# Preparation moved into the steps of a first attention, and one product moved in a second

## The chip, the cores and the metric

One core of a Trainium2 chip runs the whole program. The metric is the device time of one execution in microseconds. Times and clocks below come from one profiled execution of the kernel before, unless the runs are named.

## The reference, cut to what matters

Eight sequences of 512 tokens with 128 features pass four layers, each with a layer norm ahead and a sum behind:

```python
x = x + attn_a(layernorm(x), w_q, w_k, w_v1, w_v2)   # one head of 64, causal softmax
x = x + ffn(layernorm(x), Wg, W1, W2, W3)            # 8 experts of 352, top 2 of the scores x @ Wg.T
x = x + attn_b(layernorm(x), Q, K, V, W)             # 16 heads of 64, causal softmax
x = x + ffn(layernorm(x), Wg, W1, W2, W3)            # the same weights again
```

An expert computes `silu(x W1^T) * (x W2^T)` and multiplies by `W3^T`; its weight is the score. Everything is float32, and the products are made with pairs: a value is split into a high part (rounded for the fast product, written by ScalarE) and a low part (the rest, by VectorE), and three passes (high x high, high x low, low x high) are summed.

## The kernel before, in words

`build` runs five blocks one after the other: `prepare`, `attention_a`, `experts`, `attention_b`, `experts`. Inside a block each engine has its own instruction list, written out by hand; the lists meet only at semaphores. A list is executed in order, so what stands behind a waiting instruction waits too. At a block's end all engines meet.

**prepare** (L171 to L370). SyncE (L235) issues the loads: x by sequence, the small weights of the first attention, Wg, W1, W2, then Q, K, V, W as `[128, 64, 16]` with rows of 64 bytes, and after seven groups W3 into the place of W1's raw data. GpSimd sets constants and makes `rstd` of the norm (L134, L136). VectorE makes statistics (L123, L127), applies the norm (L146), and writes low parts (L165, L331, L335). TensorE turns `xn` (L154) and the weights by groups of four tiles (L367). ScalarE writes high parts (L160, L349, L352). Eight sequences are normalised in a loop, then Q, K, V are split directly, then come 21 groups: Wg, W1 and W2 (six each), W3 (six), W (two).

**attention_a** (L814). Steps s = -1 to 11. In step s run: scores of sequence s, projections q and k of s + 1, products with the values of s - 1, output of s - 2, and the routing of s - 3 for the experts. Routing is: moments and `rstd` (L447 to L460), `shift` (L466), the rows' norm (`route_apply`, L473), their turn (L649), scores (L664), rank (L683 to L695), count (L706, L709), place (L728 to L742, the last result is `slot`), and eight scatters by GpSimd (L754) to `x_sorted` in DRAM. Before that, SyncE stores zeros over all of `x_sorted` (the blanks, L866), and the scatters of a sequence wait for its chunk. Every result that ScalarE and VectorE split passes a `Ring` of three PSUM banks (L373): the list `order` names the fills in TensorE's order, and a fill waits (`ring_free`) until the fill three places before has been read by its last reader, mostly VectorE's low part.

**experts** (L1028, and again at the end) waits for the table (L810) and the scatters, and works through 142 tiles.

**attention_b** (L1236). 128 heads, one a slot u, in pairs. TensorE's list in a slot is: scores of u, values in two of four slots, in even slots the projection of the next pair, parts of routing, `products(u - 2)` (L554), the first turn of u - 1 (L485), in odd slots `output` of the pair behind (L81 to L83 into `z_bank`), the second and third turn. ScalarE copies each turned part (`b_pt_hi`, L414) between its exponentials (L545), VectorE writes the low parts (`b_pt_lo`, L420) and the maxima (L537), GpSimd multiplies by 1/sum (L1389). The products wait for the low part of the third turn. For the first pair of a sequence, `output` waits for `x_done`: VectorE has added `z_bank` of the sequence before to x (L1577), which it does in slot 5 of 16 of that sequence, behind the third maximum.

```python
def output(pair):
    b, p = divmod(pair, NP)
    pe.wait_ge(y_lo_done, pair + 1)
    if p == 0:
        wait(pe, x_done, b)
    three_passes(nc, z_bank[:], [w[:, p * P:p * P + P] for w in g.b_w], [part[:] for part in y_parts],
                 p == 0, p == NP - 1).then_inc(z_full, 1)
```

Of the kernel before, what the change touches and what calls it, by code (L numbers as in the profile page):

```python
# [4 lines left out]
F32 = mybir.dt.float32  # L5
# [6 lines left out]
P = 128  # L12
# [158 lines left out]
def prepare(nc, g, ins):  # L171
# [3 lines left out]
    with ExitStack() as ctx:  # L175
        sb = lambda n, s, d: ctx.enter_context(nc.sbuf_tensor(n, s, d))
        pb = lambda n: ctx.enter_context(nc.psum_tensor(n, [P, 512], F32))
        n = Norm(nc, ctx, "n0")
        a_raw = sb("a_raw", [P, 3, P], F32)
        v2_raw = sb("v2_raw", [P, D], F32)  # L180
        wg_raw = sb("wg_raw", [NE, D], F32)
        wg_rest = sb("wg_rest", [P, NE], F32)
        f_raw = [sb("f_raw0", [P, NE * HW], F32), sb("f_raw1", [P, EC * P], F32)]
        w3_raw = f_raw[0]
        qkv_raw = [sb(f"qkv_raw{i}", [P, KD, NH], F32) for i in range(4)]
        w_perm = sb("w_perm", [P, NH * KD], F32)
        sem = lambda n: g.spent.append(ctx.enter_context(nc.semaphore(n))) or g.spent[-1]
        norm_bank = [pb(f"norm_bank{i}") for i in range(2)]
        bank = [pb(f"prep_bank{i}") for i in range(4)]
        x_in = [sem(f"x_in{b}") for b in range(NB)]  # L190
        a_in = sem("a_in")
        wg_in = sem("wg_in")
        f_in = [sem(f"f_in{i}") for i in range(3)]
        b_in = [sem(f"b_in{i}") for i in range(4)]
# [4 lines left out]
        perm_done = sem("perm_done")  # L199
        padded = sem("padded")  # L200
        turned = sem("turned")
        turned_hi = sem("turned_hi")
        turned_lo = sem("turned_lo")
# [8 lines left out]
        for i, (parts, scale) in enumerate(((g.b_q, 1.0 / 128), (g.b_k, 1.0), (g.b_v, 1.0))):  # L212
            raw = qkv_raw[i][:].rearrange("p q h -> p h q")
            hi, lo = (part[:].rearrange("p (h q) -> p h q", h=NH) for part in parts)
            direct.append((raw, scale, hi, lo, b_in[i], 16))


        by_tile = lambda part: part.rearrange("p (k w) -> p k w", w=P)
        groups = [([(wg_raw[:], g.ident[0:NE, 0:NE], NE)], wg_in, 16, g.wg[:].unsqueeze(1), wg_rest[:].unsqueeze(1))]
        for i, parts in enumerate((g.w1, g.w2)):  # L220
            for j in range(0, EC, 4):
                m = min(4, EC - j)
                groups.append(([(f_raw[i][:, (j + k) * P:(j + k) * P + P], g.ident[:], P) for k in range(m)], f_in[i], 16,
                               *(by_tile(part[:, j * P:(j + m) * P]) for part in parts)))
# [1479 lines left out]
```

## Time and profile before

| | |
|---|---|
| median of 3 runs | 1491.33 us (1491.08 to 1492.69) |
| the profiled execution | 1491.82 us, of which the span of its instructions is 1490.1 us |
| mean granted clock of TensorE | 0.919 |
| busy: TensorE, VectorE, ScalarE, GpSimd | 81%, 74%, 64%, 51% of the span |
| TensorE clock in 40 equal slices | `9986656999959999999999999999999998599996` |
| share of the DMA engines in 40 slices | `9391011222125656555555556565555652122215` |
| stores of zeros in the first attention | 64, 260 KB each |

A slice is 37.3 us; a digit is tenths, 9 is 90% or more. The first two slices are the preparation, the next four the first attention, with the zeros stored in slices two and three. The clock digits 5 and 6 stand in the first attention's later half and at two changes of stage; slices 12 to 33 are the long attention. A granted clock of 1.00 is 2.4 GHz, 0.50 is 1.2 GHz, and a number between them is the mean of a stretch with both.

### The profile page before, as it was taken

What the parts mean: (1) busy time and instruction counts of PE and PEld (TensorE: products, weight loads), DVE (VectorE), ACT (ScalarE), POOL (GpSimd) and SP (SyncE); (2) the same over time, 40 slices, a digit from 0 to 9 for tenths busy, and PEclk for the clock granted to TensorE, in tenths of its full rate; (3) what the DMA queues carried; (4) which work ended last, traced back from release to release, by engine and by line L of the source; (5) the groups of instructions that cost most, each with busy time, mean ns of one, the idle gap of its engine ahead of it and who ended that gap; (6) DMA issues with size and microseconds to landing.
All of it is one profiled execution on the core that took longest, in us unless ns stands there. A gap on an engine that the chain in (4) does not pass through costs nothing. (4 is left out here: it accounts for less than half of the span.)

```text
span 1490.1 us, 28115 instructions
## 1 busy us (share of the span) xinstructions
PE 1212.1 (81%) x7865; PEld 1037.6 (70%) x7865; DVE 1099.0 (74%) x2826; ACT 946.7 (64%) x2522; POOL 757.9 (51%) x950
## 2 busy tenths in 40 slices
PE   1587734999928898988998999999999997299992
PEld 1476633999817777777777777777777776199992
DVE  5666534777727788888888888888888886277774
ACT  1554421444418788888888888889898886154440
POOL 3004463444405555576575576675765765334443
PEclk9986656999959999999999999999999998599996
DMA  9391011222125656555555556565555652122215
GB/s 182 102 379 61 29 38 45 62 60 61 40 71 128 142 128 140 130 133 139 125 129 136 127 136 141 131 153 128 135 135 127 139 131 47 31 63 60 61 52 175
DMA packets 122658, 165.15 MB, mean 111 GB/s; under 512 B 40164, under 2 KB 84079, under 8 KB 122512
## 3 DMA queue, kind: packets, MB, share of 16 engines
q1 hardware_dynamic: 109648, 144.34, 41.1%
q0 software_dynamic: 8640, 16.93, 3.6%
q10 hardware_dynamic: 4224, 2.10, 0.5%
q8 instruction: 71, 1.16, 0.3%
q14 instruction: 75, 0.61, 0.1%
HBM read 26.59 MB, written 36.96 MB: 43 GB/s over the span
## 5 line engine op out<-in xcount | busy, mean ns | idle before, releaser
L1389 POOL TENSOR_TENSOR b_probs<-b_probs,b_recip 128x128 f32<-128x128 f32 (+3 forms) x512 | 352.1, 717 | 294.8 <-DVE b_recip L1622 294.8
L420 DVE TENSOR_TENSOR b_pt_lo<-b_ring,b_pt_hi 128x512 fp32r<-128x512 f32 (+1 forms) x384 | 229.7, 598 | 104.1 <-ACT b_pt_hi L414 101.7
L545 ACT ACTIVATE b_probs<-b_s_bank,b_neg_max 128x256 f32<-128x256 f32 (+3 forms) x512 | 266.2, 530 | 47.9 <-DVE b_neg_max L537 47.9
L1227 POOL DMA_INDIRECT y_rows<-f_y_sb,f_dest x142 | 138.8, 978 | 193.0 <-DVE f_y_sb L1200 185.2
L537 DVE TENSOR_REDUCE b_neg_max<-b_s_bank 128x1 f32<-128x256 f32 (+3 forms) x512 | 219.2, 479 | 11.1 <-PE b_s_bank L529 10.9
L1437 PE MATMUL b_s_bank<-b_stack 128*128 128x256 f32 (+3 forms) x1024 | 208.0, 338 | 13.8 <-DMA b_stack<-b_qk 7.5
L414 ACT ACTIVATE b_pt_hi<-b_ring 128x512 fp32r<-128x512 f32 (+1 forms) x384 | 204.8, 534 | 14.4 <-PE b_ring L485 11.3
L485 PE MATMUL b_ring<-ident,b_probs 128*128 128x128 f32 x1280 | 190.4, 281 | 13.3 <-DVE b_qk L420 12.6
L554 PE MATMUL b_pv_bank<-b_pt_hi,b_v 128*128 128x512 f32 (+3 forms) x512 | 161.4, 327 | 45.8 <-DVE b_pt_lo L420 45.5
L1170 ACT ACTIVATE f_hid_hi<-f_hid_bank 128x384 fp32r<-128x384 f32 x142 | 69.8, 491 | 160.1 <-PE f_hid_bank L1123 135.3
L485 PEld LDWEIGHTS b_ring<-ident,b_probs 128*128 128x128 f32 x1280 | 140.6, 141 | 41.6 <-DVE b_qk L420 21.1
L1437 PEld LDWEIGHTS b_s_bank<-b_stack 128*128 128x128 f32 x1024 | 139.4, 191 | 24.8 <-ACT b_probs L545 9.8
L554 PE MATMUL b_pv_bank<-b_pt_lo,b_v 128*128 128x512 f32 (+3 forms) x512 | 146.4, 323 | 0.0
L554 PEld LDWEIGHTS b_pv_bank<-b_pt_hi,b_v 128*128 128x128 f32 x512 | 96.7, 189 | 65.2 <-DVE b_pt_lo L420 57.2
L1206 DVE TENSOR_TENSOR f_hid_lo<-f_hid_bank,f_hid_hi 128x384 fp32r<-128x384 f32 x142 | 79.2, 558 | 61.9 <-ACT f_hid_hi L1170 61.8
L1135 PE MATMUL f_y_bank<-w,f_hid_hi 128*128 x426 | 116.4, 342 | 3.7 <-DVE f_y_sb L1200 2.9
L545 ACT ACTIVATION_READ_ACCUMULATOR b_probs<-b_s_bank,b_neg_max 128x1 f32 x512 | 107.5, 210 | 0.0
L554 PEld LDWEIGHTS b_pv_bank<-b_pt_lo,b_v 128*128 128x128 f32 x512 | 96.9, 189 | 7.8
L1135 PEld LDWEIGHTS f_y_bank<-w,f_hid_hi 128*128 128x128 f32 x426 | 79.9, 188 | 25.6 <-issue 21.2
L754 POOL DMA_INDIRECT x_sorted<-a_r_rows,a_r_slot x64 | 62.3, 974 | 67.4 <-DVE a_r_slot L742 51.0
L1137 PE MATMUL f_y_bank<-w,f_hid_lo 128*128 x426 | 94.9, 223 | 0.0
L414 ACT ACTIVATE b_qk<-b_ring 128x512 fp32r<-128x512 f32 x128 | 72.5, 593 | 32.0 <-DMA b_stack<-b_qk 21.8
(298 smaller groups left out, 3024.2 us busy)
## 6 DMA issues: line engine op xcount, KB each, us to landing
b_stack<-b_qk SPq DMA_DIRECT2D x128, 384.0 KB, 5.0
b_stack<-b_qk SPq DMA_DIRECT2D x128, 256.0 KB, 4.8
x_sorted<-a_blank SPq DMA_DIRECT2D x64, 260.0 KB, 3.5
b_stack<-b_qk SPq DMA_DIRECT2D x128, 128.0 KB, 4.9
f_xs<-x_sorted SPq DMA_DIRECT2D x142, 65.0 KB
b_yc<-y_rows SPq DMA_DIRECT2D x16, 256.0 KB, 4.2
f_yc<-y_rows SPq DMA_DIRECT2D x16, 256.0 KB, 5.1
y_rows<-f_y_sb,f_dest POOLq DMA_INDIRECT x142
```

The costliest lines, as they stand in the source:

```text
L414: nc.scalar.activation(dst, src(rg.of(key)), ACT.Copy).then_inc(rg.hi_done, 1)
L420: nc.vector.tensor_tensor(dst, src(rg.of(key)), hi.bitcast(F32), ALU.subtract).then_inc(rg.lo_done, 1)
L485: last = nc.tensor.transpose(rg.of(keys[k])[:, to:to + P], probs[:, P_AT[i] + j * P:P_AT[i] + j * P + P], ident[:])
L537: nc.vector.tensor_reduce(sc.neg_max[:, i:i + 1], s_tile(sc, i), AX.X, ALU.max, negate=True).then_inc(sc.max_done, 1)
L545: nc.scalar.activation(probs[:, P_AT[i]:P_AT[i] + (i + 1) * P], s_tile(sc, i), ACT.Exp, bias=sc.neg_max[:, i:i + 1], accum_out=sums[:, i:i ...
L554: last = nc.tensor.matmul(pv_bank[:, j * P:T], v_at(j), pt[part][:, PT_AT[j]:PT_AT[j] + T - j * P], start=(j == 0 and part == 0), stop=(j ...
L1135: nc.tensor.matmul(y_bank[:, 0:2 * P], hi[:, c * P:c * P + P], w3[:, bass.ds(at, 2 * P)], start=c == 0, stop=False)
L1137: last = nc.tensor.matmul(y_bank[:, 0:P], lo[:, c * P:c * P + P], w3[:, bass.ds(at, P)], start=False, stop=c == HC - 1)
L1206: nc.vector.tensor_tensor(lo[:], hid_bank[i % 2][:, 0:HW], hi[:].bitcast(F32), ALU.subtract).then_inc(hid_lo_done, 1)
L1227: nc.gpsimd.indirect_dma_start(out=g.y_rows, out_offset=bass.IndirectOffsetOnAxis(dest[:, i:i + 1], 0), in_=y_sb[i % NY][:], in_offset=Non ...
L1389: nc.gpsimd.tensor_tensor(part, part, recip[:, i:i + 1].to_broadcast([P, (i + 1) * P]), ALU.mult).then_inc(probs_done, 1)
L1437: nc.tensor.matmul(s_tile(sc, i), stack[u % 2][:, 0, i * P:i * P + P], stack[u % 2][:, part, 0:(i + 1) * P], start=(i == S_GROUPS[group][0 ...
```

## The change

Of `prepare`, only the constants, the first attention's own weights and the norm of sequence 0 stay, with the issues of the loads of x, Wg, W1 and W2. The norms of sequences 1 to 7, the turns and splits of Wg, W1, W2, W3 and W, the splits of Q, K, V and the loads of Q, K, V, W and W3 go into the steps of `attention_a`: Wg ahead of all, three groups a step in steps 3 to 8 (`group(s, j)`), Q and K after step 9's routing, W and V in step 10. They use the ring of `attention_a` (its `order` grows accordingly). The loads of W3 and then Q, K, V, W are issued by SyncE behind all blanks. The lists of all five engines in a step are in a new order.

TensorE's list in a step (s before and after; the waits are inside the named functions):

```diff
             def body(s):
+                if s == NB + 2:
+                    permuted(0)
+                    permuted(1)
                 if live(s):
-                    scores(s)
-                if live(s + 1):
-                    project(s + 1)
+                    scores(s, 0)
+                    scores(s, 1)
+                if 0 < s + 1 < NB:
+                    norm_turn(s + 1)
+                if live(s - 2):
+                    output(s - 2)
+                if group(s, 0) is not None:
+                    weights(group(s, 0))
+                if live(s):
+                    scores(s, 2)
+                if live(s - 3):
+                    route_turn(nc, pe, g, rt, rg, s - 3)
                 if live(s - 1):
                     products(s - 1)
                 if live(s - 3):
-                    route_turn(nc, pe, g, rt, rg, s - 3)
-                if live(s - 2):
-                    output(s - 2)
+                    route_score(nc, pe, g, rt, rg, s - 3)
+                if live(s + 1):
+                    project(s + 1)
                 if live(s):
                     values(s)
                 if live(s - 3):
-                    route_score(nc, pe, g, rt, rg, s - 3)
+                    route_count(nc, pe, g, rt, rg, s - 3)
+                for j in (1, 2):
+                    if group(s, j) is not None:
+                        weights(group(s, j))
                 if live(s):
                     pe.wait_ge(sc.exp_done, s * QT + QT)
                     for k in range(len(PT_BANKS)):
                         head_transpose(nc, pe, rg, turns(s), probs, k, g.ident)
-                if live(s - 3):
-                    route_count(nc, pe, g, rt, rg, s - 3)
```

VectorE's new list in a step:

```diff
+                if s == NB + 2:
+                    for i in range(2):
+                        split_lo(nc, dve, rg, ("wb", i), perm_group(i)[1][1], perm_group(i)[1][0], in_tiles(4))
+                if 0 < s + 1 < NB:
+                    norm_apply(s + 1)
+                if live(s - 1):
+                    head_transposed_lo(nc, dve, rg, turns(s - 1), pt, 0)
+                    head_transposed_lo(nc, dve, rg, turns(s - 1), pt, 1)
                 if live(s - 3):
                     shift(nc, dve, g, rt.m, s - 3)
...
+                if live(s - 1):
+                    head_transposed_lo(nc, dve, rg, turns(s - 1), pt, 2)
+                if live(s):
+                    head_max(nc, dve, sc, s, 0)
+                if 0 < s + 1 < NB:
+                    split_lo(nc, dve, rg, ("norm", s + 1), g.xn_lo[:, tokens(s + 1)], g.xn_hi[:, tokens(s + 1)])
+                if live(s):
+                    head_max(nc, dve, sc, s, 1)
+                if live(s - 2):
+                    add(s - 2)
+                if group(s, 0) is not None:
+                    weights_lo(group(s, 0))
+                if live(s):
+                    head_max(nc, dve, sc, s, 2)
+                if live(s - 2):
+                    moments(nc, dve, g, rt.m, s - 2, x_done, (s - 1) * QT)
+                if live(s - 3):
+                    route_scored(nc, dve, g, rt, rg, s - 3)
+                if 0 < s + 2 < NB:
+                    norm_stats(s + 2)
+                if live(s - 3):
+                    route_rank(nc, dve, g, rt, rg, s - 3)
...
                 if live(s - 3):
                     route_place(nc, dve, g, rt, rg, s - 3)
-                if live(s - 2):
-                    add(s - 2)
-                    moments(nc, dve, g, rt.m, s - 2, x_done, (s - 1) * QT)
+                for j in (1, 2):
+                    if group(s, j) is not None:
+                        weights_lo(group(s, j))
+                if s == NB + 1:
+                    dve.wait_ge(b_in[3], 16)
+                    nc.vector.tensor_scalar(w_perm.rearrange("p (h v) -> p h v", h=NH),
...
```

GpSimd's list, and SyncE's added loads:

```diff
+            for s in range(-2, NB + 3):
+                if live(s - 2):
+                    rstd(nc, pool, g, rt.m, s - 2)
+                if live(s - 3):
+                    pool.wait_ge(blanked[(s - 3) % 2], ((s - 3) // 2 + 1) * NE * 16)
+                    for j in range(0, 6):
+                        route_scatter(nc, pool, g, rt, s - 3, j)
+                if 0 < s + 3 < NB:
+                    norm_rstd(s + 3)
+                if live(s - 2):
+                    route_dest(nc, pool, g, rt, s - 2)
+                if live(s - 3):
+                    for j in range(6, NK * QT):
+                        route_scatter(nc, pool, g, rt, s - 3, j)
...
+            ring_filled(sp, rg, ("w", 5))
+            sp.dma_start(w3_raw.rearrange("p (e h) -> p e h", e=NE)[:, :, 0:EH],
+                         W3.rearrange("e d h -> d e h")).then_inc(g.f_in[3], 16)
+            ring_filled(sp, rg, ("v", 3))
+            for i, w in enumerate((Q, K, V)):
+                sp.dma_start(qkv_raw[i], w.rearrange("q d h -> d q h")).then_inc(b_in[i], 16)
+            sp.dma_start(qkv_raw[3], W).then_inc(b_in[3], 16)
```

ScalarE's list puts the second and third copy of the turns of s - 1, the norm's high part, `route_apply`, the first group and `route_turned` ahead of the exponentials; q, y and k stand behind the second exponential group, and groups two and three and the first copy of the turns at the end.

In the long attention, TensorE's list:

```diff
+                if pair_behind(u, 5) is not None:
+                    output(pair_behind(u, 5))
                 if alive(u - 2):
                     products(u - 2)
                 if alive(u - 1):
                     pe.wait_ge(probs_done, u * QT)
                     head_transpose(nc, pe, rg, turns(u - 1), probs[(u - 1) % 2], 0, g.ident)
-                if pair_behind(u, 5) is not None:
-                    output(pair_behind(u, 5))
-                if alive(u - 1):
                     head_transpose(nc, pe, rg, turns(u - 1), probs[(u - 1) % 2], 1, g.ident)
                     head_transpose(nc, pe, rg, turns(u - 1), probs[(u - 1) % 2], 2, g.ident)
```

The experts are untouched.

## Rows read from the trace of the kernel before

**Rows 1.** Windows by stage: stretch, length, busy by engine, clock, DMA share, GB/s

```profile
16.40:68.10 51.70, 21.86 (x105) 17.51 (x105) 38.22 (x115) 20.21 (x31) 8.76 (x15) 0.97 0.67 108
68.10:93.30 25.20, 22.90 (x152) 18.95 (x152) 16.02 (x31) 16.29 (x45) 0.53 (x1) 1.00 0.96 353
93.30:185.30 92.00, 72.20 (x378) 62.60 (x377) 54.61 (x193) 40.09 (x105) 37.45 (x42) 0.68 0.32 113
185.30:227.40 42.10, 16.23 (x83) 15.01 (x81) 17.14 (x85) 8.89 (x19) 27.53 (x30) 0.50 0.12 38
449.00:1262.00 813.00, 740.02 (x4810) 616.11 (x4810) 690.65 (x1581) 693.04 (x1864) 507.87 (x653) 0.99 0.57 131
```

**Rows 2.** Timeline at the two ends of the preparation: start, us, instruction, idle before

```profile
11.45 4.39 SPq L250 DMA_DIRECT2D f_raw<-in_L_ffn_W_dram  x2
...
16.24 0.66 DVE L165 TENSOR_TENSOR xn_lo<-norm_bank,xn_hi 128x512 f32 x1
...
66.55 1.28 DVE L335 TENSOR_TENSOR wb_w_lo<-prep_bank,wb_w_hi 128x512 fp32r<-128x512 f32 x2
...
68.11 0.53 POOL L873 MEMSET a_blank<- 128x520 f32 x1 [14.22 <-POOLq L175]
```

**Rows 3.** Windows of 4 us over the loads; columns as in rows 1

```profile
20.00:24.00 4.00, 1.13 (x5) 0.71 (x4) 2.92 (x15) 0.67 (x2) 1.29 (x3) 1.00 1.10 269
24.00:28.00 4.00, 1.12 (x4) 0.72 (x4) 2.87 (x14) 0.82 (x2) 1.35 (x4) 1.00 1.64 114
```

**Rows 4.** Instruction groups of VectorE until 68.1 us: count, busy us, mean ns, idle before

```profile
L146 DVE TENSOR_SCALAR n_xn<-x_tok,n_mv,n_rstd 128x128 f32 (+1 forms) x32 | 8.9, 342 | 2.3 <-POOL n_rstd L136 2.3
...
L123 DVE BATCH_NORM_STATS2 n_stats<-x_tok 128x6 f32 (+1 forms) x32 | 7.0, 283 | 2.0 <-DMA x_tok<-in_L_attn_a_x_dram 2.0
L165 DVE TENSOR_TENSOR xn_lo<-norm_bank,xn_hi 128x512 f32 (+1 forms) x8 | 5.5, 688 | 7.1 <-ACT xn_hi L160 7.1
...
L127 DVE BATCH_NORM_AGGREGATE n_mv<-n_stats 128x2 f32<-128x6 f32 x32 | 3.0, 156 | 0.3
```

**Rows 5.** Timeline: the last slot of the first attention

```profile
227.20 0.21 DVE L742 TENSOR_REDUCE a_r_slot<-a_r_of_place 128x8 int32<-128x64 f32 x1
```

**Rows 6.** Window of one step with routing; columns as in rows 1

```profile
130.00:148.00 18.00, 13.84 (x78) 11.47 (x77) 10.81 (x39) 7.97 (x21) 9.03 (x10) 0.69 0.09 30
```

**Rows 7.** Timeline: turns by TensorE at a granted clock of 0.50

```profile
108.71 2.37 PE L485 MATMUL a_ring<-ident,a_probs 128*128 128x128 f32 x10
```

**Rows 8.** Waits, 449 to 1233 us: who for whom, total us, times, longest

```profile
PE b_pv_bank L554 <- DVE b_pt_lo L420: 38.7, 55, 1.2
...
ACT b_qk L414 <- DMA b_stack<-b_qk: 20.2, 21, 2.8
...
PE b_z_bank L81 <- DVE x_tok L1577: 9.5, 7, 1.4
```

**Rows 9.** Timeline of an ordinary odd slot of the long attention

```profile
820.69 0.50 PE L554 MATMUL b_pv_bank<-b_pt_hi,b_v 128*128 128x512 f32 x1 [0.34 <-DVE b_pt_lo L420]
...
822.01 0.63 PE L485 MATMUL b_ring<-ident,b_probs 128*128 128x128 f32 x4
...
822.68 0.60 ACT L414 ACTIVATE b_pt_hi<-b_ring 128x512 fp32r<-128x512 f32 x1
```

**Rows 10.** Timeline of slot 5 of a sequence in the long attention

```profile
984.10 0.50 PE L554 MATMUL b_pv_bank<-b_pt_hi,b_v 128*128 128x512 f32 x1 [0.29 <-DVE b_pt_lo L420]
...
986.66 0.68 DVE L1577 TENSOR_TENSOR x_tok<-x_tok,b_z_bank 128x512 f32<-128x512 f32 x1
986.67 0.60 ACT L414 ACTIVATE b_pt_hi<-b_ring 128x512 fp32r<-128x512 f32 x1
...
987.49 0.47 PE L81 MATMUL b_z_bank<-b_y_hi,wb_w_hi 128*128 128x512 f32 x1 [1.43 <-DVE x_tok L1577]
...
988.90 0.60 ACT L414 ACTIVATE b_pt_hi<-b_ring 128x512 fp32r<-128x512 f32 x1 [0.96 <-PE b_ring L485]
```

**Rows 11.** Timeline: the first instruction behind the first attention

```profile
243.57 0.16 POOL L1221 MEMSET f_dest<- 128x71 int32 x1 [5.54 <-POOLq L830]
```

More of the change, by code:

```diff
@@ L356, in _ @@
             pe.wait_ge(consts, 16)
[L357 to L368 removed]
+            norm_transpose(nc, pe, g, n, 0, norm_bank)
 class Ring:
@@ L391, in of @@
         return self.bank[self.at[key] % len(self.bank)]
-HI_ONLY = ("rows",)
+HI_ONLY = ("rows", "wg")
 LO_ONLY = ("scores", "counts", "table")
@@ L811, in plan_table, with attention_a, group @@
     nc.vector.tensor_scalar(pl.valid[:], bank[:, 2 * P:3 * P], g.index[:, 0:1], None, ALU.is_gt).then_inc(pl.table_done, 1)
-def attention_a(nc, g, pl):
+def attention_a(nc, g, pl, ins):
+    Q, K, V, W, W3 = ins[5], ins[6], ins[7], ins[8], ins[12]
+    NG, PER = 18, 3
     turns = lambda b: [("turn", b, k) for k in range(len(PT_BANKS))]
-    order = []
-    for s in range(-1, NB + 4):
+    def group(s, j):
+        return PER * (s - 3) + j if s >= 3 and 0 <= PER * (s - 3) + j < NG else None
+    order = [("wg", 0)]
+    for s in range(-1, NB + 3):
+        if s == NB + 2:
+            order += [("wb", 0), ("wb", 1)]
+        order += [("norm", s + 1)] if 0 < s + 1 < NB else []
+        order += [("w", group(s, 0))] if group(s, 0) is not None else []
+        order += [("rows", s - 3), ("scores", s - 3)] if live(s - 3) else []
         order += [("q", s + 1), ("k", s + 1)] if live(s + 1) else []
-        order += [("rows", s - 3)] if live(s - 3) else []
         order += [("v", s)] if live(s) else []
-        order += [("scores", s - 3)] if live(s - 3) else []
+        order += [("counts", s - 3)] if live(s - 3) else []
+        order += [("w", group(s, j)) for j in (1, 2) if group(s, j) is not None]
         order += turns(s) if live(s) else []
-        order += [("counts", s - 3)] if live(s - 3) else []
     order += [("table", 0)]
@@ new lines, in norm_turn, with weights @@
+            def norm_turn(b):
+                pe.wait_ge(n_xn_done, b * QT)
+                ring_free(pe, rg, ("norm", b))
+                for t in range(QT):
+                    last = nc.tensor.transpose(rg.of(("norm", b))[:, t * P:t * P + P], n_xn[:, t * D:t * D + D], g.ident[:])
+                last.then_inc(rg.filled, 1)
+            def weights(i):
+                pe.wait_ge(g.f_in[1 + i // 6], 16)
+                if i // 6 == 2:
+                    pe.wait_ge(padded, 1)
+                ring_free(pe, rg, ("w", i))
+                for k, src in enumerate(weight_group(i)[0]):
+                    last = nc.tensor.transpose(rg.of(("w", i))[:, k * P:k * P + P], src, g.ident[:])
+                last.then_inc(rg.filled, 1)
@@ L895, in project, with permuted @@
+            def permuted(i):
+                pe.wait_ge(perm_done, 1)
+                ring_free(pe, rg, ("wb", i))
+                for k, src in enumerate(perm_group(i)[0]):
+                    last = nc.tensor.transpose(rg.of(("wb", i))[:, k * P:k * P + P], src, g.ident[:])
+                last.then_inc(rg.filled, 1)
             def project(b):
+                if b:
+                    pe.wait_ge(rg.lo_done, rg.lo["norm", b])
                 for name, w in (("q", g.a_wq), ("k", g.a_wk)):
```

275 lines of the change are left out of this document (145 added, 130 removed).

## The prediction

> **What bounds the kernel now.** I first cut the span into stages [rows 1] and asked of each which engine has no idle time and what ends the idle time of the others. The reader should see five stages. Until 16.4 us only sequence 0 is normalised, its low part `xn_lo` last [rows 2]. From 16.4 to 68.1 us the kernel prepares: VectorE is busy for 38.2 of 51.7 us, TensorE for 21.9, and nothing of the attention runs. From 68.1 to 227.4 us the first attention runs, its last `slot` at 227.2 us [rows 5]. The experts follow, and from 449 us the long attention, where the span mostly goes: 813 us with TensorE at 91%, VectorE and ScalarE at 85%, so no engine has much room there and the order decides. In the first attention it is otherwise. Until 93.3 us (steps 0 to 2, TensorE at full clock) VectorE is busy 16.0 of 25.2 us; in the next 92.0 us, five steps with routing, only 54.6, and the clock is 0.68; in the last 42.1 us (steps 8 to 10) 17.1, the clock at 0.50. One such step of 18.0 us has 10.8 us of VectorE and 8.0 of ScalarE in it [rows 6]: it is bound by a chain across engines (place, add, moments, `rstd` on GpSimd, shift, rows, turn, scores, rank, count, place) and not by work. So the preparation stage is a stretch that can be covered, and the first attention has idle time to cover it with.
>
> **The change in the first attention.** *Start.* The part that stays in `prepare` ends with `xn_lo` of sequence 0. Before, that split ran at 16.24 us, behind the statistics of sequence 1 [rows 2]; without them it can follow `xn_hi` at once, by about 15.8. SyncE is then the last: its last load of W1 and W2 is issued at 15.84 [rows 2]. With 0.3 us for the change of blocks (as from 67.83 to 68.11 before) and some slack, the attention's first instruction comes at 16.4 instead of 68.1: 51.7 us less. Everything else is what comes back into the steps.
>
> *Added work of VectorE.* For one sequence: four statistics 0.87, four aggregates 0.38, four applications 1.11, one low part 0.69, together 3.0 us; for one weight group, which has the shape of the latter, again 0.69 [rows 4], busy time over eight sequences. With three groups, a step of 3 to 5 gets 3.0 + 2.1 = 5.1 us. ScalarE gets a copy of 0.6 us for each, 2.4 in such a step, on top of 8.0: it stays under VectorE. GpSimd gets 1.25 us beside 9.0 [rows 6]. Its queue is passed in order: `norm_rstd` of sequence s + 3 stands between the sixth and the seventh scatter and waits for statistics that VectorE makes a step later, so two scatters and the next `rstd` wait behind it. Their result is wanted at the next step's head; by my count of the instructions between, VectorE has 7 us of work in that time and GpSimd 5: covered, by 2 us.
>
> *Steps -1 to 2.* They get 1.2 + 3 x 3.0 = 10.2 us of VectorE, and had 9.2 idle [rows 1]. But `norm_apply` stands at the head of the step, and project(s + 1) now waits for turn, high and low part of the same sequence. I take 7.5 us more (0 if all falls into idle time; 15 if ScalarE's and TensorE's parts, 0.6 and 1.1 us for each of three, are added in full too).
>
> *Steps 3 to 7.* VectorE has 10.8 + 5.1 = 15.9 us in steps 3 to 5. The new order puts shift and application first, the sums and moments in the middle and place last, so that the routing chain of one sequence lies beside scores and products of another; I take the fill that the long attention reaches with such an order, 0.86 of the time there (0.85 with its ends, [rows 1]), so 18.5 us each. Step 6 has no statistics left: 14.6 / 0.86 = 17. Step 7 has no norm and no q, k: 11.5 / 0.86 = 13.4; the old step took 18.5; the mean, 16. Together 88.5 instead of 92.0: 3.5 less. Bounds: 74 (VectorE never idle) and 113 (the old time plus all that is added).
>
> *Steps 8 to 10.* 17.1 us of VectorE plus three groups (2.1), w_perm (1.1), three direct low parts (1.9 each) and two groups of W: 27.3, or 31.7 at 0.86. The old time is 42.1, where the clock of 0.50 and the serial chain count; the mean, 37: 5 less. Bounds 32 and 52.
>
> *Loads.* x, W1 and W2 (5 MB) come at some 270 GB/s until about 24 us [rows 3], and the blanks (64 x 260 KB) queue behind them; at the 353 GB/s of before [rows 1] they end near 72 us. The first scatter is due at about 66 and needs only the first chunk. W3 and Q, K, V, W follow the blanks on SyncE's queue and are wanted in steps 7 and 9: hidden by two steps or more. If that cover went, the four strided loads (2 MB at 114 GB/s, [rows 3]) would cost some 18 us once.
>
> Sum: -51.7 + 7.5 - 3.5 - 5.1 = **-52.8 us**; the stretch behind the last slot (scatters, table) stays.
>
> *The clock.* TensorE has 1.00 granted in steps 0 to 2, where it is busy for 22.9 of 25.2 us, and 0.68, then 0.50, later, where it waits longer [rows 1]. The five steps get four turns for the norm and twelve for the weights, so its waits get shorter, and I expect it nearer to 1.0. The Trainium skill ("TensorE: Matmul & The Clock Gate", "HAM oscillation — how this bites in real kernels") says that idle gaps between bursts throw TensorE back to its lower clock; the trace agrees, and by that rule the added work half pays for itself.
>
> **The change in the long attention.** In odd slots `output(pair)` (three products of 512 columns, 0.70 us) moves from behind the first turn to in front of `products`. *What it fills:* TensorE stands 38.7 us in 55 slots at the products, waiting for `pt_lo` [rows 8]; the output now runs in that time. *What it delays:* the ScalarE copy of the first turn starts as soon as that turn ends in most odd slots [rows 9]: products wait 0.34 us, start at 820.69, and ScalarE starts at 822.68, 0.04 after the turn's end. With the output in front they start 0.36 later, and so does ScalarE. Over all odd slots, 0.70 minus the wait where that is positive, less the slack of 0.6 us that 14 of the 62 have in the timeline, comes to 7 us. *What it gives back:* all of TensorE's work after the second turn is earlier by the filled wait, up to 0.6 us a pair, which shortens ScalarE's waits for the stack's DMA (20.2 us in all, [rows 8]) and for turns; I take a third, 9 us.
>
> *The added wait.* For the first pair of a sequence, `output` waits for `x_done`, the sum of the sequence before; seven such waits, 9.5 us [rows 8]. Row by row [rows 10]: products start at 984.10, the copy of the first turn at 986.67, the sum is made at 986.7 and the output starts at 987.49. After the change the products are queued behind that wait: output 987.49 to 988.2, products to 989.6, first turn to 990.2. ScalarE's copy comes 3.6 us later, its exponential of 0.7 after it, and the second copy at 991.5 instead of 988.90 (which now needn't wait for its turn): the slot grows by **2.6 us**. Seven times: 18. Bounds: 0, if the following slots take it up; 25 (7 x 3.6) if nothing is regained.
>
> Sum: 7 - 9 + 18, taken as **+15.5 us** (bounds -15 and +28).
>
> Together -52.8 + 15.5 = -37.3 on the profiled execution's 1491.8 us (span 1490.1 and 1.7 around it), which is 0.5 over the median: **1454.0 us**.
>
> **The rivals.**
> *A, the wait for `x_done` is taken up* (0.2). For it: after the stall TensorE has the second turn ready at once, and later slots have TensorE waits. Against: ScalarE and VectorE are the loop that sets the slot. Then 1491.3 - 52.8 - 2 = 1436 us.
> *B, half of VectorE's moved work is not covered* (0.2). The old stage's idle time is idle because of a chain, and the ring of three banks, which now passes 20 more fills, ties the three engines together. Of 38 us moved 19 come back and nothing is won in the steps: 1491.3 - 51.7 + 19 + 15.5 = 1474 us.
> *C, the block of `prepare` ends only when the loads of W1 and W2 have landed* (0.1): then the attention starts near 24 us [rows 3] and the change does not do what its start says; 7.5 us more, 1461 us. At the end of the first attention, where scatters are under way, the next block does start 5.5 us late [rows 11].
> *D, slower: TensorE stays at its lower level and becomes the bound* (0.05). A step's 13.8 us of TensorE at a mean clock of 0.69 [rows 6] are 19.1 at 0.50, and the sixteen turns added, at 0.24 us each there (ten in 2.37 us, [rows 7]), 3.8: 22.9, and with the 4.2 us that TensorE now waits in a step, 27. For steps 3 to 8 that is 6 x 27 = 162 instead of 100 in my sum (88.5 and 12): 1454 + 62 = 1516 us. It decides from about 24 us a step on. Against it: a TensorE busy for 91% of the time had the full clock in both places where that was so [rows 1].
>
> **How the numbers follow.** My forecast, 0.45, holds 1440 to 1468. The predicted time is its own. Range 1430 to 1480: it takes in A to C and leaves out D, B's worse half and a first attention filled better than 0.86 together with A. A measurement of this kernel can tell about 0.2%, 3 us, from no change: faster 0.94 (all but D and a piece of B), slower 0.05, the same 0.01.
>
> **What would show it.** Right: `a_blank` is set near 16.4 us; scores of step 3 near 49 us; slots every 18.5, later 16 and 12 us, the last near 174 us; granted clock above 0.8 in steps 3 to 7; in the long attention TensorE idles before the `z_bank` product and not before `pv_bank`, seven slots of a sequence's head are 2.6 us longer and others equal. Wrong: a start at 24 us (C), steps over 20 us with VectorE below 75% (B), a clock of 0.5 with TensorE above 90% (D), no longer head slots (A). Most would go wrong with the ring: if a fill waits for a low part that stands late on VectorE, all three engines stop, which none of my sums has priced.

## The result

The changed kernel takes **1478.64 us** (median of 4 runs, 1477.18 to 1479.69) against 1491.2 us (1489.81 to 1492.69) of the kernel before: a ratio of 0.9915, with a 95% interval of 0.9898 to 0.9932. It is 12.6 us faster where I forecast 37. The sign and the range held, the size didn't: a third of the forecast gain is there. The range held with nothing to spare, 1.4 us inside its upper end.

Windows by stage of the changed kernel: stretch, length, busy by engine (TensorE, its weight loads, VectorE, ScalarE, GpSimd), granted clock, DMA share, GB/s. The stretches answer to those of [rows 1]: steps -1 to 2, steps 3 to 7, steps 8 to 10, and the long attention from its first 1/sum to its last.

```profile
16.40:49.00 32.60, 27.54 (x168) 22.65 (x168) 29.21 (x97) 19.40 (x50) 6.35 (x10) 0.97 1.06 360
49.00:136.20 87.20, 68.83 (x434) 60.38 (x434) 68.98 (x244) 48.51 (x118) 42.09 (x48) 0.83 0.67 149
136.20:177.10 40.90, 20.43 (x115) 18.16 (x114) 27.05 (x84) 19.33 (x32) 29.32 (x29) 0.58 0.12 38
401.20:1236.40 835.20, 761.19 (x4781) 616.66 (x4780) 687.87 (x1574) 688.08 (x1855) 502.37 (x646) 0.98 0.56 127
```

The same stretch of the long attention in the kernel before:

```profile
449.50:1251.40 801.90, 733.27 (x4780) 610.41 (x4780) 686.32 (x1573) 688.16 (x1854) 501.83 (x646) 1.00 0.58 132
```

The reader sees a first attention whose last `slot` ends 50.3 us earlier (177.1 against 227.4), and a long attention that is **33 us longer** with VectorE and ScalarE busy for the same time to 2 us. TensorE is busy for 28 us more with the same instructions, and its clock fell from 1.00 to 0.98. So the first part came nearly as forecast, and most of it was given back in the second. The waits of the long attention in the changed kernel (who for whom, total us, times, longest) say where:

```profile
PE b_z_bank L81 <- DVE x_tok L1691: 20.8, 7, 3.1
```

```profile
ACT b_pt_hi L329 <- PE b_ring L400: 36.2, 13, 5.5
```

The seven waits for `x_done` went from 9.5 [rows 8] to 20.8 us, and ScalarE's waits for turned parts, the first turn behind such a wait among them, went from 8.9 to 36.2 us (13 waits in both) and now reach 5.5 us. One of them in the timeline (start, us, instruction, idle before), beside [rows 10]:

```profile
957.69 0.68 DVE L1691 TENSOR_TENSOR x_tok<-x_tok,b_z_bank 128x512 f32<-128x512 f32 x1
...
958.52 0.77 PE L81 MATMUL b_z_bank<-b_y_hi,wb_w_hi 128*128 128x512 f32 x1 [2.97 <-DVE x_tok L1691]
...
959.08 0.63 PE L82 MATMUL b_z_bank<-b_y_lo,wb_w_hi 128*128 128x512 f32 x1
...
959.94 0.63 PE L469 MATMUL b_pv_bank<-b_pt_hi,b_v 128*128 128x512 f32 x1
...
961.98 1.28 PE L400 MATMUL b_ring<-ident,b_probs 128*128 128x128 f32 x10
...
962.64 0.60 ACT L329 ACTIVATE b_pt_hi<-b_ring 128x512 fp32r<-128x512 f32 x1 [4.82 <-PE b_ring L400]
```

The wait of 2.97 us is as worked out. What isn't in my sum is the duration behind it: a product of 512 columns takes 0.63 us, where it takes 0.40 at the full clock (L82 in the lines of e5 below). TensorE came out of the wait at half its clock.

### The profile page after: what moved, and what is told of

Same layout as the page of the kernel before. It is cut to its first block and busy times, and to the rows that moved or that the text cites. A ratio compares the mean times of both kernels' runs of the same rounds, so it can differ in the third digit from the quotient of the medians.

```text
span 1476.9 us, 28006 instructions
## 1 busy us (share of the span) xinstructions
PE 1224.8 (83%) x7865; PEld 1032.5 (70%) x7865; DVE 1099.4 (74%) x2819; ACT 948.5 (64%) x2522; POOL 762.3 (52%) x949
## 5 line engine op out<-in xcount | busy, mean ns | idle before, releaser
L1552 PE MATMUL b_s_bank<-b_stack 128*128 128x256 f32 (+3 forms) x1024 | 211.5, 340 | 19.1 <-DMA b_stack<-b_qk 10.0
L1552 PEld LDWEIGHTS b_s_bank<-b_stack 128*128 128x128 f32 x1024 | 140.5, 192 | 35.5 <-DMA b_stack<-b_qk 15.5
L469 PE MATMUL b_pv_bank<-b_pt_lo,b_v 128*128 128x512 f32 (+3 forms) x512 | 150.4, 330 | 0.0
L469 PEld LDWEIGHTS b_pv_bank<-b_pt_hi,b_v 128*128 128x128 f32 x512 | 99.8, 195 | 41.5 <-DVE b_pt_lo L335 32.3
L469 PEld LDWEIGHTS b_pv_bank<-b_pt_lo,b_v 128*128 128x128 f32 x512 | 100.0, 195 | 9.0
L1742 DVE TENSOR_TENSOR b_y<-b_pv_bank,b_y 64x512 f32<-64x512 f32 x128 | 87.4, 683 | 4.1 <-ACT b_y L1663 2.2
```

Of the source, the lines that this page charges most:

```text
L469: last = nc.tensor.matmul(pv_bank[:, j * P:T], v_at(j), pt[part][:, PT_AT[j]:PT_AT[j] + T - j * P], start=(j == 0 and part == 0), stop=(j ...
L1552: nc.tensor.matmul(s_tile(sc, i), stack[u % 2][:, 0, i * P:i * P + P], stack[u % 2][:, part, 0:(i + 1) * P], start=(i == S_GROUPS[group][0 ...
L1742: nc.vector.tensor_tensor(y[row:row + KD, :], pv_bank[0:KD, :], y[row:row + KD, :], ALU.add).then_inc(y_done, 1)
```

## The experiments

The texts put down ahead of each run name theories by a letter. In the first group T says that the added wait makes the loss, R that what the first attention leaves behind makes it, S that moving the output costs by itself.

**Whose order costs what.** First, each part alone, and two ways to take only the wait away, all on one chip, where the kernel before took 1493.0 us.

e1 puts the old order back into the long attention:

```diff
-                if pair_behind(u, 5) is not None:
-                    output(pair_behind(u, 5))
                 if alive(u - 2):
                     products(u - 2)
 ...
                     head_transpose(nc, pe, rg, turns(u - 1), probs[(u - 1) % 2], 0, g.ident)
+                if pair_behind(u, 5) is not None:
+                    output(pair_behind(u, 5))
+                if alive(u - 1):
 ...
```

> The kernel after with the long attention's TensorE list as it was before (output behind the first turn); the first attention stays changed. Theory T: the gain of the first attention (its last slot came 50.3 us earlier) is all there, and it was given back in the long attention by the wait for the sum of x in front of the products, whose seven occurrences make the 33 us by which that stage is longer. Then this kernel takes 1491.2 - 49 = 1442 us, 1440 to 1446, and the long attention is 802 us from its first to its last reciprocal. Rival R: the long attention is slower because of what the first attention leaves (placement of data, DMA, clock); then it stays near 835 us and the time near 1475.

Measured: 1455.03 us, ratio 0.9738 (0.9709 to 0.9767), 38 us faster than the kernel before, not 49, and above the 1440 to 1446 expected; its long attention 807.4 us. Theory T holds for 27.6 of the 33 us; 5.5 us stay with the order of before, so R isn't all wrong. The other half of the missing 11 us is in the first attention: with the same code its last slot is at 182.2 us here, 5.3 later than in the result's trace.

e2 is the kernel before with that diff turned round: the new order of the long attention, and nothing else.

> The kernel before with the new TensorE list of the long attention alone. Theory T: the order alone costs what the long attention lost in the changed kernel, 33 us: 1524 us, 1519 to 1528. Rival R (cost from what the first attention leaves): about 1491. My forecast's own sum of this part was +15.5: 1507.

Measured: 1518.16 us, ratio 1.0167 (1.014 to 1.0195): the new order alone makes the old kernel **slower by 25 us**, its long attention 826.5 instead of 801.9. That is just under T's 1519 to 1528, whose 33 us had the 5.5 of e1 in them. The two ratios multiply to 0.990, the result's 0.9915 to within their intervals: the parts add up.

e3 keeps the output in front for seven pairs of eight:

```diff
+                behind = pair_behind(u, 5)
+                if behind is not None and behind % NP != 0:
+                    output(behind)
 ...
                     head_transpose(nc, pe, rg, turns(u - 1), probs[(u - 1) % 2], 0, g.ident)
+                if behind is not None and behind % NP == 0:
+                    output(behind)
+                if alive(u - 1):
 ...
```

> The kernel after, but the output of the first pair of a sequence (which waits for the sum of x) stands behind the first turn as before; the seven other pairs keep it in front of the products. Theory T: all of the loss is the wait, and the move of the other pairs is worth about nothing or a little (my forecast had 7 lost, 9 won): 1441 us, 1437 to 1446. Rival S: the move itself costs in every odd slot, by the delay of ScalarE's copy (my forecast's 7 us, without what it gives back) or more: 1450 and above.

e4 leaves the output in front and moves VectorE's sum, from behind the three maxima to ahead of them:

```diff
             for u in slots:
+                if leaving(u, Z_ADD) is not None:
+                    added(leaving(u, Z_ADD))
                 if alive(u):
                     head_max(nc, dve, sc, u, 0)
 ...
-                if leaving(u, Z_ADD) is not None:
-                    added(leaving(u, Z_ADD))
```

> The kernel after, with VectorE's sum of x put ahead of the three maxima of slot 5 instead of behind them; the output stays in front of the products. Its input was ready before the slot began, so the sum ends at about 1.4 us after the slot's start instead of 4 and TensorE doesn't wait. Theory T: the loss is that wait and the fall of TensorE's clock behind it: 1442 + 7 x 0.7 at most for maxima that come later, so 1442 to 1448. Rival S (the move of output costs by itself): 1455 and above.

Measured: e3 1453.58 (0.9724, 0.9694 to 0.9754), e4 1452.87 (0.9721, 0.9693 to 0.9749); long attention 807.8 and 807.1 us against e1's 807.4. e1 and e3 are 13 us over the times that I wrote, e4 5 to 11, and e3's time taken by itself lies where S expected it. But e1, which moves no output, is as long, and the three agree with one another: S falls, the move of 56 outputs is worth 0.4 us (e3's long attention against e1's), and seven waits make all of the 27 us.

**What the seven waits cost.** In the changed kernel's own trace one of the seven waits, that of 3.12 us at 533.4 us, was not followed by a fall of the clock. The 3.2 us behind the output's start in the next sequence (first line) and in this one (second):

```profile
638.50:641.70 3.20, 3.18 (x9) 2.72 (x10) 0.00 (x0) 0.00 (x0) 0.00 (x0) 0.50 0.63 157
533.40:536.60 3.20, 3.19 (x22) 2.98 (x23) 0.00 (x0) 0.54 (x2) 0.00 (x0) 1.00 0.56 134
```

Nine instructions at 0.50, twenty-two at 1.00. A slot is measured from one 1/sum of VectorE to the next. Here are those around the wait with the full clock, in the changed kernel,

```profile
527.84 0.18 DVE L1736 RECIPROCAL b_recip<-b_sums 128x4 f32<-128x4 f32 x1
537.36 0.18 DVE L1736 RECIPROCAL b_recip<-b_sums 128x4 f32<-128x4 f32 x1
544.01 0.18 DVE L1736 RECIPROCAL b_recip<-b_sums 128x4 f32<-128x4 f32 x1
```

and in the kernel before:

```profile
574.01 0.18 DVE L1622 RECIPROCAL b_recip<-b_sums 128x4 f32<-128x4 f32 x1
580.05 0.18 DVE L1622 RECIPROCAL b_recip<-b_sums 128x4 f32<-128x4 f32 x1
587.80 0.18 DVE L1622 RECIPROCAL b_recip<-b_sums 128x4 f32<-128x4 f32 x1
```

The slot with the full clock took 9.51 us, those with a fall 10.5 to 11.6, where the kernel before has 6.05; the slot behind is back from 7.74 to 6.65 us (in the last sequence, whose slots are shorter, from 7.34 to 6.09). So the wait by itself is 9.51 + 6.65 - 6.05 - 7.74 = 2.4 us, and a fall 1.4 to 2.1 more (the last sequence's slot is 9.01 us without one, in e5 below; the smallest price of a fall, in e8, is 0.9). The Trainium skill ("TensorE: Matmul & The Clock Gate", "HAM oscillation — how this bites in real kernels") says that gaps between bursts bring the slower clock back; the traces agree, though the gaps of its example are longer than most of these: in the three traces with waits of 2.7 to 3.4 us at this place (changed, e2, e8), 18 of 21 were followed by it, and none of the 35 waits of 0.92 to 1.44 us in the five of the old order (before, e1, e6, e9, e10), nor of the 14 of up to 1.48 us in e3 and e7.

The length of one wait doesn't decide alone. At other places of the long attention seven falls stand behind waits of 1.73 to 2.00 us, one of them in e5:

```profile
639.57 1.03 PE L400 MATMUL b_ring<-ident,b_probs 128*128 128x128 f32 x6 [1.82 <-DVE b_qk L335]
```

e10 and e11 have a fall each behind a wait of 1.19 us with two shorter ones ahead of it, while 2.10 us in e7 and 2.29 us in e8 kept the clock at 1.00.

The second group ran on another chip, where the kernel before took 1485.65 us, with the changed kernel again as e8. Theory C says that the fall of the clock is part of the price; N that only the wait counts; P that the price goes with the wait's length. e5 fills the wait with products whose result is overwritten:

```diff
+                behind = pair_behind(u, 5)
+                if behind is not None and behind % NP == 0 and behind > 0:
+                    wait(pe, y_done, u - 2)
+                    for k in range(11):
+                        nc.tensor.matmul(pv_bank[:], g.b_w[0][:, 0:P], g.b_q[0][:, 0:T], start=True, stop=True)
                 if pair_behind(u, 5) is not None:
                     output(pair_behind(u, 5))
```

> The kernel after, with 11 products of 512 columns into the free bank of the products, whose result is overwritten, put in front of the output that waits for the sum of x, seven times in all. In the changed kernel TensorE stands there for 3.0 us and its granted clock is 0.50 for the 3.2 us behind, so the output, the products and the first turns take about 1.6 us longer than at 1.00. Theory C (the fall of the clock is part of the price): the wait itself stays, the clock stays at 1.00, each of the seven slots is 1.5 us shorter than in the changed kernel: 10 us less than it in the same call. Rival N (only the wait counts, the slower products are taken up later): no change, or some us more for the added products.

e7 shortens the wait by putting VectorE's sum between its maxima:

```diff
                     head_max(nc, dve, sc, u, 1)
+                if leaving(u, Z_ADD) is not None:
+                    added(leaving(u, Z_ADD))
+                if alive(u):
                     if u % VQ < 2:
 ...
-                if leaving(u, Z_ADD) is not None:
-                    added(leaving(u, Z_ADD))
```

> The kernel after, with VectorE's sum of x in slot 5 between its second maximum and the low part of the values, where VectorE waits 0.4 us for ScalarE anyway. By the changed kernel's rows the sum then ends near 1.25 us after TensorE comes to the output, instead of 3.0. Theory C (price = wait + fall of the clock, and the clock doesn't fall behind a wait this short, as it didn't behind the 1.44 us of the kernel before): the slot loses 1.3 us instead of 4.6, so seven of them are worth 20 us or more against the changed kernel: 1453 to 1460. Rival P (the price is proportional to the wait): 1.3/3.0 of 27 us stays, 12 us over e3's 1453.6: 1463 to 1467.

> The kernel after, unchanged, as the yardstick on the chip of e5 and e7: 0.9915 of the kernel before, some 1478 to 1481 us, in the long attention 3.0 us of wait in each of seven slots. Both theories expect the same.

Measured: e8 1454.9 (0.9802, 0.9771 to 0.9833), far under the 1478 to 1481 that I wrote ("The other chip", below), e5 1448.2 (0.9751, 0.9721 to 0.978), e7 **1434.64** (0.966, 0.963 to 0.969). In e5 TensorE still waits for VectorE, but comes out of it at full speed:

```profile
930.70 2.79 PE L1603 MATMUL b_pv_bank<-wb_q_hi,wb_w_hi 128*128 128x512 f32 x11
...
934.41 0.47 PE L81 MATMUL b_z_bank<-b_y_hi,wb_w_hi 128*128 128x512 f32 x1 [0.93 <-DVE x_tok L1696]
...
934.72 0.40 PE L82 MATMUL b_z_bank<-b_y_lo,wb_w_hi 128*128 128x512 f32 x1
```

Six of its seven slots took 9.51 to 9.53 us: the number of the slot above without a fall, where e8 has 10.4 to 11.6 but for one, 9.51. That is theory C. The 10 us that I wrote were 6.7, since the falls of e8 come to 8 us only, those of the result's trace to 10. The seven slots are 7.8 us shorter than e8's; the slots just ahead of them are 4.9 longer, before the added products run, in four of them with ScalarE waiting ahead of its copies of q and k, and others are shorter, so that the whole time alone would be a weak witness. e7 has a wait of 1.26 us and the full clock:

```profile
924.44 0.67 DVE L1691 TENSOR_TENSOR x_tok<-x_tok,b_z_bank 128x512 f32<-128x512 f32 x1
...
925.25 0.47 PE L81 MATMUL b_z_bank<-b_y_hi,wb_w_hi 128*128 128x512 f32 x1 [1.26 <-DVE x_tok L1691]
```

It is 20.3 us under e8, and its slots of 7.81 and 6.64 are together 0.7 us over the old pair's 13.79, which makes 5 us for seven. P, which had 12 of 27 us stay, falls. With e11 and e12 (below) the price can be read off: the two slots take 12.70 us where nothing waits (e11), and 3.46, 1.75 and 0.77 us more with a wait of 2.97, 1.26 and 0.28 us at the full clock. Each is the wait plus 0.5 us; that this is the output's own 0.7 less some idle time that it fills is my reading. The fall of the clock comes on top of the longest alone.

**Who sets the steps of the first attention.** e6 is e1 with VectorE's low part of each weight group made twice. Rival B2 is that the chain across engines and the clock set these steps and that VectorE's work is covered:

```diff
-                split_lo(nc, dve, rg, ("w", i), parts[1], parts[0], in_tiles(len(tiles)))
+                key = ("w", i)
+                dve.wait_ge(rg.hi_done, rg.hi[key])
+                wait(dve, twice_done, i)
+                nc.vector.tensor_tensor(twice[:, 0:len(tiles) * P].rearrange("p (k w) -> p k w", w=P), in_tiles(len(tiles))(rg.of(key)),
+                                        parts[0].bitcast(F32), ALU.subtract).then_inc(twice_done, 1)
+                split_lo(nc, dve, rg, key, parts[1], parts[0], in_tiles(len(tiles)))
```

> e1 (the kernel after with the long attention's old order) with the low part of each of the 18 weight groups made a second time by VectorE into a spare place: 18 x 0.69 = 12.4 us more of VectorE in steps 3 to 8 of the first attention, nothing else changed. My forecast's fill of 0.86 says that VectorE sets steps 3 to 5, and a mean of work and old time steps 6 and 7: then the last slot comes 12.4 / 0.86 = 14 us later at most, 8 to 14, and the time is 1463 to 1469 against e1's 1455. Rival B2 (the steps are set by the chain across engines and the clock, and VectorE's work is covered): 0 to 4 us later, under 1460.

Measured: 1444.99 us (0.9724, 0.9696 to 0.9753), and the last slot at 170.1 us, where the six runs that share the rest of this stage on such chips (e5, e7, e8, e10, e11, e12) have it at 156.2 to 159.1. That is 12.5 us later than their mean, 11.0 to 13.9 by the single one, for 12.4 us of work: work added to VectorE's list lengthens these steps one for one. B2 falls, on this kind of chip; on the result's, where VectorE is idle for more of these steps, it wasn't tried. (The times that I wrote, 1463 to 1469, were for a chip like that of e1.) It doesn't make rival B right: with the moved work in them these steps take 74.3 us on such a chip (below), and the old ones took 92.0 without it.

**The other chip.** e8 is the changed kernel, word for word, and it is 31 us faster than the kernel before where the result has 13. Its last slot is 17.8 us earlier; 12.9 of these lie in steps 3 to 7, 5.1 in steps 8 to 10. e8's windows of steps 3 to 7 and 8 to 10, and its slots (count, min/median/max ns, first and last start), with the changed kernel's slots below:

```profile
49.00:123.30 74.30, 64.29 (x436) 57.15 (x436) 68.53 (x247) 47.67 (x120) 42.12 (x48) 0.85 0.80 175
123.30:159.10 35.80, 18.37 (x116) 15.86 (x114) 26.55 (x82) 19.35 (x32) 28.86 (x28) 0.64 0.13 42
```

```profile
L657 DVE TENSOR_REDUCE a_r_slot<-a_r_of_place x8: 207/209/209, 62.8 to 159.1; 128x8 int32<-128x64 f32 x8
```

```profile
L657 DVE TENSOR_REDUCE a_r_slot<-a_r_of_place x8: 207/208/209, 62.6 to 176.9; 128x8 int32<-128x64 f32 x8
```

The same VectorE work (68.5 and 69.0 us) fills 92% of 74.3 us in one and 79% of 87.2 us in the other. Where the rest goes is seen in two like places: in the changed kernel, TensorE's turn of the routing rows and ScalarE's copy of it,

```profile
125.23 0.61 PE L564 MATMUL a_ring<-ident,a_r_rows 128*128 128x128 f32 x4
...
130.44 0.60 ACT L329 ACTIVATE a_r_xn_t<-a_ring 128x512 f32<-128x512 f32 x1 [3.70 <-remote]
```

and in e8:

```profile
102.20 0.66 PE L564 MATMUL a_ring<-ident,a_r_rows 128*128 128x128 f32 x4
...
102.95 0.60 ACT L329 ACTIVATE a_r_xn_t<-a_ring 128x512 f32<-128x512 f32 x1 [0.32 <-PE a_ring L564]
```

ScalarE starts 0.1 us or less behind the turn's end in e8 in each of the eight sequences, but 2.9, 3.2, 5.3 and 4.6 us behind it in steps 4 to 7 of the result's trace, idle for 2.3, 2.6, 4.7 and 4.0 of these. TensorE meanwhile starts its next instructions at the same pace (the ends of its instructions are modelled in these traces). From 62 to 140 us ScalarE and VectorE stand for 17.7 and 8.3 us in waits for which the profile names no releaser ("remote", "issue"); in e8 for none.

The third group, on a third chip (1484.27 us for the kernel before), asked whether that goes with the chip; theory H says that it does, by signals of TensorE that come late on some. e9 is the kernel before, e10 is e1, e12 is e4, and e11 is e10 with e4's diff.

> The kernel before, unchanged, for a trace on the same chip as the next three. In the two groups of runs so far the changed kernel stood 12.6 us under the kernel before in one and 31 us in the other, and the difference lies in the first attention: its last slot at 176.9 us in one and 159.1 us in the other, with ScalarE and VectorE idle for 26 us between 62 and 140 us without a releaser in the one and not at all in the other. Theory H (TensorE's signals come late on some chips, and a chain of short steps pays for it, the kernel before less than the one after): the last slot is at 227 us or a few us earlier here, whichever the chip.

> e1 again (first attention changed, long attention's old order). On a chip like that of e1: 0.974 of the kernel before, last slot near 182 us. On one like that of e5 to e8: last slot near 159 us, and 0.966 to 0.969 of the kernel before (e8's 0.980 less 27 us of the wait gives 0.962). Theory H expects one of the two, and that the two differ by the idle time without a releaser in steps 4 to 8; a rival, that e8's first attention was faster by chance of one execution, expects something between.

> e10, with VectorE's sum of x put ahead of the maxima of slot 5. In the old order the output waits 1.44 us for that sum behind the first turn, seven times, and the slot behind is 7.75 us where others of its kind take 6.65. Theory T: this wait goes, and with it up to 1.1 us, less 0.7 for the later maxima: 0.3 to 0.5 us seven times, 2 to 4 us less than e10.

> e4 again (output in front, sum ahead), beside e11, which differs from it only in where the output of a pair stands. Theory T: where nothing is waited for, the place of the output is worth nothing, 0 to 2 us (my forecast had 2 for the pairs without a wait): e11 and e12 within 2 us. Rival S (the move itself costs or gains): more than 4 us between them.

Measured: e9 1483.44 (1.0003), e10 1430.75 (0.9626, 0.9583 to 0.9669), e11 **1423.38** (0.9578, 0.9538 to 0.9619), e12 1428.65 (0.9611, 0.9568 to 0.9654). e9's last slot is at 223.7 us, 3.5 earlier than in [rows 5], e10's at 156.2 where e1 has 182.2. (e10's 0.9626 is below the 0.966 to 0.969 that I wrote, and at the 0.962 of the sum beside it.) So it isn't the chance of one execution: it goes with the chip, or with the group of runs, each of which had one chip. That late signals of TensorE are behind it is a reading. The six traces of the two kernels and of e1 to e4 have such waits (25.5 us of ScalarE's in the kernel before from 93 to 227 us, 0 in e9), none of the eight of e5 to e12. Where they occur the kernel before loses 3.5 us in its first attention, the kernels with the changed one 18 to 26. I have no run that tells what makes the signals late. The six traces also record fewer semaphore events, 19.0 to 19.4 thousand each against 22.3 to 22.4 thousand in the eight; from 75 to 100 us, 233 in the changed kernel and 350 in e8. A missing record may by itself leave a wait without a named releaser, but not make the idle time. The Trainium skill ("NOTIFIC — the notification-queue block", "Overflow: three behaviours, one of which stalls the engine") says that a full queue of such records can, by its setting, drop new records, write over old ones or stall what produces them; no run here shows which of these happened, if any.

e11 beats both kernels: 0.9578 of the kernel before, where e8 has 0.9802 on the same kind of chip, 33 us less than the changed kernel. Its output stands behind the first turn, and VectorE's sum is made before anyone asks for it:

```profile
914.47 0.67 DVE L1692 TENSOR_TENSOR x_tok<-x_tok,b_z_bank 128x512 f32<-128x512 f32 x1
...
916.31 0.48 PE L81 MATMUL b_z_bank<-b_y_hi,wb_w_hi 128*128 128x512 f32 x1
```

No idle time stands before the product. e11 gains 7.4 us on e10, more than the 2 to 4 that I wrote: the maxima that come 0.7 us later cost nothing (the slot stays at 6.05), and the 1.1 us of the slot behind come whole. e12 is 5.3 us over e11, where T had at most 2 and rival S more than 4: by the number S is right. The slots say where: in the seven its output still waits 0.3 to 0.5 us for the sum, and with its own 0.7 us holds up the first turn (6.82 against 6.05, together 5.4 us). All other slots of the long attention together are 0.7 us shorter in e12, so outside the seven the place of the output is worth next to nothing, as T had it.

## Why the prediction was wrong

By the two profiled executions the span shrank by 13.2 us, and I had forecast 37.3. The 24 us between them, in the order of my sum:

- **Start: right.** The first attention's first instruction is at 16.48 us, forecast 16.4. Rival C falls: the block doesn't wait for the loads of W1 and W2.
- **Steps -1 to 2: right.** 32.6 us against 25.2 + 7.5 = 32.7; scores of step 3 at 49.
- **Steps 3 to 7: right in number, by luck.** 87.2 us, forecast 88.5. Two errors cancel: VectorE is busy for 69.0 us where I had counted 74, and the fill of 0.86 taken from the long attention is 0.79 here. On e8's chip the fill is 0.92 and the steps take 74.3 us, which only looks like my lower bound of 74, since that stood for more work and no idle time. The order was better than I credited, and the chip of the result took it back. The granted clock is 0.83, as expected above 0.8; D falls.
- **Steps 8 to 10:** 40.9 us against 37, a miss of 4 on this chip, 35.8 on the other. Together the last slot is 50.3 us earlier, not 52.8: 2.5 us of the 24.
- **Behind the last slot: a step missing.** I let the stretch behind it stay. It lost 2 us until the long attention and 2 more behind it.
- **The wait for `x_done`: the mechanism right, the term mis-sized. This is the step that failed.** The row by row working gave 2.6 us for the slot. The slot without a fall grew by 3.5, and the one behind it gave 1.1 back, since it had held the old wait: 2.4 for the pair, near my number partly by luck. And I priced the work behind a wait of 3 us at the rate of [rows 10], where the wait was 1.43 us and the clock stayed. Sum of the seven head slots and those behind them: 122.2 us against 95.5, that is 26.7 instead of 18, of which 16.6 are the wait and 10.1 the clock. I had used the rule of the clock for the first attention, where it speaks for the change, and not here, where it speaks against it. A is refuted by the same rows: beyond that 1.1 us nothing is taken up later.
- **Products and outputs of other pairs: near in sum, parts not shown.** 7 lost and 9 won were forecast, -2 (and the sum, 16, was then rounded to 15.5); e3 against e1 shows +0.4. No run separates the 7 from the 9.
- **A cost that isn't in the diff:** the long attention is longer by 5.5 us in e1 against the kernel before, and by 9.4 us in e10 against e9, with not one line of it changed. I had put this term at nothing. ScalarE's idle time ahead of the copies of q and k grew with it, by 5.1 and 5.7 us: enough for the 5.5, not for the 9.4. Group of these copies (busy us, mean ns, idle before and its releasers) in the kernel before and in e1:

```profile
L414 ACT ACTIVATE b_qk<-b_ring 128x512 fp32r<-128x512 f32 x128 | 72.5, 593 | 32.0 <-DMA b_stack<-b_qk 21.8 <-PE b_ring L83 8.9
```

```profile
L329 ACT ACTIVATE b_qk<-b_ring 128x512 fp32r<-128x512 f32 x128 | 72.9, 594 | 37.1 <-DMA b_stack<-b_qk 25.3 <-PE b_ring L83 10.7
```

  The four kernels with the new first attention and the old order (e1, e6, e10, e11) have 36.0 to 37.1 us there, those with the old first attention 30.7 to 32.0, on both kinds of chip. Why ScalarE waits longer there, for the stack's transfers above all, isn't settled.

So of the 24 us, 10.1 are the clock (less 1.4 by which the wait itself was over-priced), about 9 the other slots of the long attention (of which 5.5 as in e1), 2.5 the first attention and 4 the stretches around. The first of these is shown by experiment; of the other 15 the runs show where they are and not why. On the other kind of chip e10 against e9 is -52.7 us for the first part, my -52.8, but by luck: its last slot is 67.5 us earlier, and by the two spans 13.5 of them are lost again behind it.

The single step whose correction would have helped most: a wait that grows from 1.4 to 3 us on TensorE must be priced at both clocks. With 1.4 us more in each of seven slots the forecast would have been 1464 on the chip of the result, still 15 us low; the rest was in the places that I took as unchanged.

## What to carry to other kernels

Before an instruction is put in front of others on an in-order engine, ask what it waits for in its rarest case: here 57 of 64 outputs waited for nothing, and the seven that did cost 27 us, while the free ones won nothing. Rather than move the consumer, look for the producer: VectorE's sum could be made at the slot's head at hardly any cost, and that alone was worth 7 us in the old order. And price every longer wait of TensorE twice, as idle time and as what its work behind costs at the lower clock.

## What the hardware showed that I hadn't expected

- At the first output of a sequence, waits of 2.7 to 3.4 us were followed by 3.2 us or more at a granted clock of 0.50 in 18 of 21 cases, waits of 0.92 to 1.48 us in none of 49. Elsewhere in the long attention waits of 1.7 to 2.3 us went either way. Eleven products whose result is overwritten, in front of the wait, kept the clock at 1.00 behind it in seven of seven.
- The same program has its first attention's last slot at 176.9 us on one chip and at 159.1 us on another. The kernel before differs by 3.5 us there. So the worth of a change differs by chip: 0.9915 and 0.9802 for this one. Why is open.
